# Turning the attention probabilities with VectorE block transposes and SBUF-to-SBUF transfers in place of TensorE identity products

## What is computed

```python
q = einsum('bsd,hpd->bhsp', x, q_w);  k = einsum('bsd,hpd->bhsp', x, k_w)
xv = einsum('bsd,hedp->bshep', x, v_w)
v = einsum('bshep,bshe->bhsp', xv, gate_v)
att = softmax(einsum('bhqp,bhkp->bhqk', q, k) * SCALE, axis=-1)
ctx = einsum('bhqk,bhkp->bqhp', att, v)
weighted = ctx[:, :, :, None, :] * gate_o[..., None]
out = einsum('bshep,hepd->bsd', weighted, o_w)
```

## Time and profile before

| | |
|---|---|
| median of 3 runs | 3138.77 us (3130.59 to 3141.73) |
| span of the profiled execution, first to last instruction | 3102.4 us |
| PE, DVE, ACT, POOL busy | 2958.3, 2183.4, 1926.7, 1838.9 us |
| share of the span | 95%, 70%, 62%, 59% |
| DMA | 140048 packets, 124.71 MB |
| granted TensorE clock, mean | 0.979 |

### The profile page before, as it was taken

The page is one execution under the profiler, slowest core; times in us unless marked ns, Lnnn a source line. Parts: engine busy times, 40 slices in busy tenths (PEclk is TensorE's granted clock), DMA queues, the critical chain, the costliest instruction groups (busy, mean ns, idle before and its releaser), DMA issues. The chain is left out here.

```text
span 3102.4 us, 53399 instructions
## 1 busy us (share of the span) xinstructions
PE 2958.3 (95%) x17672; PEld 2071.1 (67%) x17672; DVE 2183.4 (70%) x4152; ACT 1926.7 (62%) x4366; POOL 1838.9 (59%) x2333
## 2 busy tenths in 40 slices
PE   4999999999999999999999999999999987899998
PEld 2666666666666666666666666666667675567675
DVE  7777888877778888777788887777777655235243
ACT  1576666676667666666666666666666743353634
POOL 2466666676666666676766676666666645433330
PEclk7899999999999999999999999999999989899999
DMA  5000001100100011001000110011001011233222
GB/s 171 21 22 23 22 22 33 32 23 26 44 26 22 23 32 33 23 23 37 29 22 22 33 32 23 23 37 29 23 22 40 16 42 44 65 96 104 86 77 87
DMA packets 140048, 124.71 MB, mean 40 GB/s; under 512 B 28662, under 2 KB 122304, under 8 KB 139680
## 3 DMA queue, kind: packets, MB, share of 16 engines
q1 hardware_dynamic: 127312, 88.75, 10.2%
q0 software_dynamic: 10160, 30.17, 3.1%
q10 hardware_dynamic: 2304, 2.36, 0.4%
HBM read 97.47 MB, written 29.28 MB: 41 GB/s over the span
## 5 line engine op out<-in xcount | busy, mean ns | idle before, releaser
L1340 DVE TENSOR_REDUCE m_peaks<-m_ring 128x1 f32<-128x512 f32 x1024 | 636.7, 681 | 95.3 <-PE m_ring L299 95.1
L1072 ACT ACTIVATE m_expA<-m_ring 128x512 f32<-128x512 f32 x1024 | 536.3, 607 | 120.5 <-PE m_ring L372 102.3
L933 POOL TENSOR_TENSOR m_vprod<-m_vprod 128x512 f32<-128x512 f32 x256 | 334.3, 1306 | 451.5 <-DVE m_vprod L1353 327.1
L1043 ACT ACTIVATE m_prob<-m_ring,m_negs 128x512 f32<-128x512 f32 x512 | 350.8, 691 | 285.9 <-DVE m_negs L1388 285.4
L943 POOL TENSOR_TENSOR m_oprod<-m_oprod 128x512 f32<-128x512 f32 x256 | 329.4, 1287 | 258.9 <-ACT m_oprod L1012 255.2
L350 PE MATMUL m_ring<-m_probT,m_vs 128*128 128x256 f32 x2048 | 464.4, 380 | 5.8 <-DVE m_vprod L1353 5.2
L350 PEld LDWEIGHTS m_ring<-m_probT,m_vs 128*128 128x128 f32 x2048 | 386.3, 190 | 68.4 <-issue 13.3
L1378 DVE TENSOR_REDUCE m_negs<-m_ring 128x1 f32<-128x512 f32 x512 | 344.3, 684 | 115.3 <-PE m_ring L105 113.2
L1353 DVE TENSOR_TENSOR m_vprod<-m_ring,m_gate 128x512 f32<-128x512 f32 x512 | 342.2, 687 | 112.4 <-PE m_ring L105 99.5
L1053 ACT ACTIVATE m_probT<-m_ring 128x512 f32<-128x512 f32 x512 | 294.0, 610 | 63.2 <-PE m_ring L338 61.8
L1012 ACT ACTIVATE m_oprod<-m_ring,m_go 128x128 f32<-128x128 f32 x1024 | 292.0, 372 | 34.6 <-PE m_ring L105 23.7
(11 more groups left out here) (322 smaller groups left out, 5558.3 us busy)
## 6 DMA issues: line engine op xcount, KB each, us to landing
m_wraw<-in_v_w SPq DMA_DIRECT2D x32, 512.0 KB, 4.1
m_qf<-q_dram SPq DMA_DIRECT2D x128, 128.0 KB, 2.7
m_wraw<-in_o_w SPq DMA_DIRECT2D x32, 512.0 KB, 4.3
q_dram<-m_kf SPq DMA_DIRECT2D x24, 256.0 KB, 4.4
listed<-in_pad SPq DMA_DIRECT2D x6, 897.0 KB, 11.5
m_xg<-listed SPq DMA_DIRECT2D x39, 138.0 KB
m_rows<-answers SPq DMA_DIRECT2D x8, 512.0 KB, 4.1
sums_dram<-m_sumsT ACTq DMA_DIRECT2D x128, 18.0 KB
```

The source lines that it names most:

```text
L933: vchain(pool.tensor_tensor(vprod[:, 0:512], vprod[:, 0:512], vprod[:, 512:1024], ALU.add))
L1043: act.activation(prob[t % 2][:, c * 512:(c + 1) * 512], ring.home["scores", n, t, c][:, :], ACT.Exp, bias=neg[t % 2], accum_out=den[n % 2] ...
L1072: act.activation(expA[hh][:, c * 512:(c + 1) * 512], ring.home["scT", n, k, hh, c][:, :], ACT.Exp)\
L1340: v.tensor_reduce(peaks[:, t, hh, c:c + 1], ring.home["peaks", n, t, hh, c][:, :], AX.X, ALU.max)\
```

## The change

`turn`, `keep_turned` and the second `probT` buffer are gone. In their place:

- DVE turns one tile of 128x1024 with one instruction, which transposes its 128 blocks of 32x32 each in place, into the new tile `turned` (`turn_probs`, 8 a step). The two tiles of a group lie side by side in it.
- SP moves the blocks to their partitions with 16 SBUF-to-SBUF DMAs for each group (`move_probs`, four calls a step), one for each pair of a block of 32 source and 32 destination partitions. Each has 32 x 8 pieces of 64 f32 numbers, 256 bytes, and 64 KB in all.
- There is one `turned` and one `probT`. A group's move waits for its two turned tiles and for `ctx_made` of the group before; `turn_probs` of an even tile waits until the move before has landed; `softmax` of tile k waits for the turning of tile k - 2; `weigh` waits for the move.
- The columns of the context come out as (a, t, j) and are put in order by the access patterns of `keep_ctx` and `lower_ctx` (`by_tile`, `by_block`).
- The left half of the outputs (c = 0) is scaled on ACT too: 8 more groups of four instructions of 128x128 a step in place of 8 `gate_outputs` on DVE (`LEFT_BY_DVE = ()`). `scale_outputs` has one call for each half.
- All five loops have new orders and run over `range(-5, N0 + 5)`. In PE's order the groups of four `peak_scores` and `scores_by_key` no longer stand together everywhere. SP's loop has the moves between its loads, and the once-a-batch loads stand between `move_probs(i, 2)` and `move_probs(i, 3)`.
- `find_largest` waits for `largest_found` of two tiles before. Layer 1's loads are issued one step earlier, and its splitting and the inversion of the early heads' sums stand elsewhere in DVE's order.

```diff
-                def turn(n, t, h):
-                    pe.wait_ge(probs_made, 2 * (TPB * n + t) + h + 1)
-                    ps = claim(ring, ("probT", n, t, h), probT_kept, 16 * n + 2 * t + h + 1)
-                    for c in range(4):
-                        last = pe.transpose(ps[:, c * P:(c + 1) * P],
-                                            prob[t % 2][:, (4 * h + c) * P:(4 * h + c + 1) * P], ident[:, :])
-                    last.then_inc(probs_turned, 1)
...
                 def weigh(n, g):
...
-                    pe.wait_ge(probT_kept, 16 * n + 4 * g + 4)
+                    pe.wait_ge(probs_moved[g % 2], moved(n, g))
...
-                        last = pe.matmul(ps[:, 0:2 * P], vs[n % 2][:, k, :], probT[g % 2][:, k, :],
+                        last = pe.matmul(ps[:, 0:2 * P], vs[n % 2][:, k, :], probT[:, k, :],
...
+                def turn_probs(n, t):
+                    k = TPB * n + t
+                    v.wait_ge(probs_made, 2 * k + 2)
+                    if t % 2 == 0 and k:
+                        v.wait_ge(probs_moved[(k // 2 - 1) % 2], moved(0, k // 2 - 1))
+                    v.transpose(turned[:, :, t % 2, :], prob[t % 2][:, :].rearrange("p (c r) -> p c r", r=32))\
+                        .then_inc(probs_turned, 1)
...
+                def move_probs(n, g):
+                    sp.wait_ge(probs_turned, 8 * n + 2 * g + 2)
+                    if 4 * n + g >= 1:
+                        sp.wait_ge(ctx_made, 4 * n + g)
+                    by_key = turned[:, :, :, :].rearrange("p (k b) t j -> p b k (t j)", b=4)
+                    for a in range(4):
+                        for b in range(4):
+                            sp.dma_start(probT[32 * b:32 * b + 32, :, 64 * a:64 * a + 64],
+                                         by_key[32 * a:32 * a + 32, b, :, :]).then_inc(probs_moved[g % 2], 16)
...
-                def keep_turned(n, t, h):
-                    act.activation(probT[g % 2][:, 4 * h:4 * h + 4, (t % 2) * P:(t % 2 + 1) * P],
-                                   ring.home["probT", n, t, h][:, :].rearrange("p (c q) -> p c q", c=4),
-                                   ACT.Copy).then_inc(probT_kept, 1)
...
-                        last = act.activation(oprod[t % 2][:, 512 + e * D:512 + (e + 1) * D],
-                                              ring.home["outputs", n, t, 1][:, e * D:(e + 1) * D], ACT.Copy,
-                                              scale=go[:, t, 4 + e:5 + e])
+                        last = act.activation(oprod[t % 2][:, c * 512 + e * D:c * 512 + (e + 1) * D],
+                                              ring.home["outputs", n, t, c][:, e * D:(e + 1) * D], ACT.Copy,
+                                              scale=go[:, t, 4 * c + e:4 * c + e + 1])
```

More of the change, by code:

```diff
@@ L46 @@
 FILLS = 6
+LEFT_BY_DVE = ()
 def spread(ap, n):
@@ L225, in layer0 @@
         den = [m.sbuf(f"den{k}", [P, TPB, 2]) for k in range(2)]
-        probT = [m.sbuf(f"probT{k}", [P, TPB, 2 * P]) for k in range(2)]
+        probT, turned = m.sbuf("probT", [P, TPB, 2 * P]), m.sbuf("turned", [P, T // 32, 2, 32])
         ctxT = [m.sbuf(f"ctxT{k}", [PS, 2, 2 * P]) for k in range(2)]
@@ L513, in _ @@
                     scores_by_key(i - 1, 4, 0, 1)
+                    sum_by_key(i - 1, 3)
+                    scores(i - 1, 5, 0)
+                    scores(i - 1, 5, 1)
                     scores_by_key(i - 1, 4, 1, 0)
+                    values(i, 3, 0)
+                    values(i, 3, 1)
                     scores_by_key(i - 1, 4, 1, 1)
[L516 to L519, removed]
+                    peak_scores(i, 4, 1, 1)
@@ L521, in _ @@
+                    scores(i - 1, 6, 0)
+                    weigh(i - 1, 1)
+                    sum_by_key(i - 1, 5)
+                    scores_by_key(i - 1, 6, 1, 1)
+                    scores(i - 1, 6, 1)
+                    values(i, 4, 0)
+                    values(i, 4, 1)
+                    outputs(i - 1, 0, 0)
                     peak_scores(i, 5, 0, 1)
@@ L523, in _ @@
                     peak_scores(i, 5, 1, 1)
[L524 to L531, removed]
                     peak_scores(i, 6, 0, 0)
+                    values(i, 5, 0)
+                    values(i, 5, 1)
+                    outputs(i - 1, 0, 1)
+                    outputs(i - 1, 1, 0)
                     peak_scores(i, 6, 0, 1)
@@ L582, in _ @@
-                    values(i + 1, 0, 1)
-                    scores(i, 2, 1)
-                    outputs(i - 1, 3, 1)
-                    weigh(i - 1, 3)
-                    turn(i, 1, 0)
-                    turn(i, 1, 1)
-                    peak_scores(i + 1, 0, 0, 0)
-                    peak_scores(i + 1, 0, 0, 1)
-                    peak_scores(i + 1, 0, 1, 0)
-                    peak_scores(i + 1, 0, 1, 1)
-                    sum_by_key(i - 1, 7)
-                    scores_by_key(i, 0, 0, 0)
@@ L693, in load_queries, with load_values @@
                             sp.dma_start(qf[rows, :], q_dram[n // HS % 2][2 * h + hh, :, :]).then_inc(q_loaded, 16)
-                def load_values(n):
+                def load_values(n, first=False):
+                    if n not in steps or n < 2 and not first:
+                        return
                     h = n % HS
@@ L704, in load_outputs @@
                 def load_outputs(n):
+                    if n not in steps:
+                        return
                     h = n % HS
```

528 lines of the change are left out of this document (265 added, 263 removed).

## The result

The changed kernel takes 3503.36 us (median of 4 runs, 3491.06 to 3506.08), the kernel before 3139.38 beside it on the same chip. The ratio is 1.116, 95% interval 1.1136 to 1.1183: 11.6% slower where 2.4% faster was predicted, and outside the range.

A forecast was written before the change was run, and what follows sets the result against it. PE was taken as the bound: its list shrinks 4.64 us a step, less 1.35 of waiting and 0.7 of clock, 2.6 saved. Over 31 steps that is 80 us, less 5 at layer 0's end: 3064 us, range 2990 to 3200.

The forecast's parts named there:

- PE is the bound: In layer 0's steps PE was busy about 75 of 76 us, so what leaves its list is time saved.
- 0.44 a turn: On PE, each of 16 turns a step costs 0.44 us, so removing them saves 7.04 us a step.
- The new order's 2.40: On PE, the new order adds 1.36 us a step for changes of kind and 1.04 for runs of 32-row products.
- ACT at nothing: ACT loses 294.0 us of evictions and gains 292.0 us of scalings, so no change; its 52 us lie under PE's list.
- A transpose takes 1.28: On DVE, a block transpose of 1,024 columns takes 1.28 us, eight a step 10.2 us; bounds 1.1 and 2.55.
- Just hidden: DVE's 40 or 47 us of work in the peaks' stretch fits PE's 43 us plus 4 from the ring of banks.
- Rival 3: DVE becomes the bound, a transpose costing 2.55 us: 77 us a step, 3165 us in all; chance 0.12.
- The move at 9.1 us: A group's 16 DMAs on SP take 6.9 us to issue, at 0.43 each, and 2.2 to land; bounds 7.3 and 12.5.
- rival 2: Moves late: pieces cost 40 ns, a move 12.5 us, `weigh` 1 is 4.75 late and `weigh` 3 2.6: 3350; chance 0.20.
- One late `weigh` a step, 1.35 us: On PE, only `weigh` 1 waits for its move, 9.1 against 7.75 us of list: 1.35 us a step.
- The clock: After an idle wait PE's clock falls, costing about 2 us; a third of it, 0.7 us a step, was counted.
- The small pieces: The move's 256-byte pieces take 19 ns each, 4.9 us a group, hidden under the issue; at 40 ns, 10.3, not hidden.

The follow-up runs named there:

- run 8: Kernel before without its turns on PE and their copies on ACT, the weighted sums reading probabilities filled once: 2980.54 us, ratio 0.9472.
- run 10: Changed kernel without moves and without transposes, the weighted sums reading probabilities filled once: 3142.05 us, ratio 0.9988 to the kernel before.
- run 1: Changed kernel without moves, transposes kept, `weigh` reading a `probT` filled once: 3258.57 us, ratio 1.0400 to the kernel before.
- run 9: Kernel before without turning, eight unread DVE transposes a step added ahead of the join of the next tile's maxima: 3203.79 us, ratio 1.0191.
- run 11: Kernel before without turning, eight unread DVE transposes a step added behind the join of the next tile's maxima: 3197.87 us, ratio 1.0166.
- run 2: Changed kernel with 8 of the 16 DMAs of each move, the rest of `probT` filled once: 3262.25 us, ratio 1.0405 to the kernel before.
- run 4: Changed kernel, all computed, each move DMA having 32 pieces of 2 KB instead of 256 of 256 bytes: 3446.06 us, ratio 1.0973.

## Why the prediction was wrong

The ratios of runs 8, 10, 1 and of the changed kernel, on 3139 us, split the 364 us. The forecast's column is its own sum, 31 steps long. "New orders" holds the left outputs' move to ACT as well, as run 10 has both:

| part | predicted, us | measured, us | a step, predicted and measured |
|---|---|---|---|
| turns leave PE | -218 | -166 | -7.04, -5.3 |
| new orders | +74 | +162 | +2.40, +5.2 |
| transposes on DVE | 0 | +129 | 0, +4.2 |
| moves | +69 | +239 | +2.05 and the tail, +7.7 |
| sum | -75 | +364 | |

By its own steps:

- *PE is the bound*: right; run 8 takes the turns from PE and their copies from ACT, which was busy 62%, and the time falls.
- *0.44 a turn*: too high by a fifth. The list's busy time fell by 75.7 - 69.8 = 5.9 us, not 7.04, and idle time rose by 0.7. That the neighbours of a turn cost something else when it is gone would explain it; no run shows it.
- *The new order's 2.40*: mis-sized, 5.1 by the windows of runs 8 and 10, which is above its own upper bound of 4.4. The term that failed first is 0.23 for a lone product, read from a duration of 393 ns. The start distance is 0.42 to 0.43 (1054.50 to 1054.93). The longer runs were wrong as well: not 0.11 for each product beyond four. In run 10's timeline one step's runs of two cost 0.43 and 0.56, of three 0.43 to 0.67, of four 0.43 to 1.02, of five 0.67, of six 1.18 and of seven 1.35. An estimate from these: the runs up to four add 1.4 us a step to the forecast, the three long ones 1.2. In the run of five at 1068.68 two pairs share their 32 rows, and two products start 0.33 us behind the other three, which fits one waiting for the other of its pair; in the run of seven the last starts a further 0.57 us late, a wait inside the run whose cause was not tested. The count was slightly off too: the last two products of a pass and the first of the next stand together, so there are 20 runs and 36 changes, not 21 and 37.
- *ACT at nothing*: right as a busy time. No run moved the left outputs alone.
- *A transpose takes 1.28*: right, 1.233, as an ordinary pass of that width (1.275). The rule of the Trainium skill (Vector Engine (DVE) Microarchitecture Reference, The reshape front-end and per-opcode configuration), one element per cycle per lane, would have it cost like one. 128 x 1,024 elements in 1.233 us are 0.83 elements a ns in each of 128 lanes; the trace has no cycles to compare.
- *"Just hidden"* on DVE: wrong, and this is the costliest sentence after the moves. I had compared DVE's work with PE's time over a stretch, 40 or 47 us against 43 and 4, and took a tie for cover. As I read runs 9 and 11, a list with a fixed order has no cover in a tie; each piece is late by what stands before it. Rival 3 expected this cost only from a transpose at half rate.
- *The move at 9.1 us*: wrong, 12.5. Landing was right (2.1 for 2.2), the pieces too (24 ns, hidden). The failed term is 0.43 an issue; it was 0.61, and 0.65 from start to start. The 0.43 was a mean over sixteen of L743's loads, one of which took 1.32 us (the largest of its line above) where the median is 0.31, so they were no slower than L270's at 0.36; the three stores at 0.61 stood in the same trace and weren't used. Run 2 shows what this is worth: a move of 7.3 us is free. That also fits rival 2, which decides from 10.5 us: its duration came true, though not by its 40 ns pieces.
- *One late `weigh` a step, 1.35 us*: two, of 2.8 us each, 5.5 a step. Rival 2 had 4.75 and 2.6; the list between `weigh` 0 and 1 was 9.1 where I had 7.75, which softened the first.
- *The clock*: the fall counted at a third came. The mean granted clock in the steady steps is 0.96, where the earlier trace rows have 1.00, and 1.00 again in the window of run 1. PE's busy time is 78.9 in place of run 1's 76.1, and a product of `weigh` takes 442 ns where it takes 380 at full clock. The 36 slowed `weigh` calls carry it, 2.8 us a step against my 0.7.
- *The small pieces*: the Trainium skill's demand for at least 512 B (DMA: Bandwidth & Descriptors, Specifications) is worth at most the 57 us of run 4, where a move has 2 KB pieces. Its other section, that SBUF-to-SBUF transfers do not suffer from small pieces, is the one that the 24 ns and run 2 agree with. Neither of the two speaks of what did decide, the issue.

For the lone product, the slack on DVE and the clock the forecast took a reading on the friendly side each time. For the issue it took the slower of its two rows, and both were the wrong kind of row. The misses of the table add up to 439 us, where 75 would have undone the gain. The rival that named the moves as late got the direction right, and its 3350 is nearest; it had neither the transposes' price nor that of the new list.

## What to carry to other kernels

Don't price a DMA issue by the first loads that resemble it in piece size: in one trace issues took from 0.31 to 0.61 us, out of SBUF too from 0.35 to 0.61, and the dearest that could apply belonged among the rivals. SP's queue set 16 x 0.65 us here, bytes and pieces little; halve the number of issues before anything else. Where engines run fixed orders through one ring, work that is put on a neighbour "in its free time" may cost much of its duration all the same: 4.2 of 9.9 us a step with DVE 71% busy before, 7.2 with 84%, by the ledger above. Before the new orders of such a change are believed, run the change's list with its new operations left out: run 10 alone would have said that nothing could be gained.

## What the runs showed of the hardware that was not expected

- The move's DMAs, issued by SP from SBUF to SBUF, take 0.59 to 0.61 us of its queue at the median (0.65 from start to start in a row), and this hardly depends on their pieces: 256 of 256 bytes, 128 of 256 bytes, or 32 of 2 KB. Other issues took 0.35 (stores out of SBUF by L733) or 0.39 (loads by L701), the latter 0.60 behind a move. What sets it stays open.
- 256-byte pieces from SBUF to SBUF go at about 24 ns each on a DMA engine, 94 GB/s at a share of 0.56, and 8 of 16 such DMAs a move beside all engines at work cost them nothing that could be measured (3262 us for 3259).
- A lone product of 32 rows by 512 columns between full-array products holds PE for 0.42 to 0.43 us, what four side by side do.
- After PE's waits for the move in the window, 1.3 to 6.3 us long, the granted clock was lower in 36 of 50 cases, and `weigh` then took 5.1 to 6.7 us in place of 3.72. The 14 cases without a fall had waits of 1.4 to 3.5 us.
